# Half down products by token tile, and a per-tile path into the token-head attention, in a two-layer hybrid kernel

## The reference

```python
# experts: top 2 of 8; for each choice e, with its low-rank terms
h  = silu(x @ W1.T + (x @ A1[e].T) @ B1[e].T) * (x @ W3.T + (x @ A3[e].T) @ B3[e].T)
y += gate[e] * (h @ W2.T + (h @ A2[e].T) @ B2[e].T)      # F = 896 = 7 chunks of 128
# heads of a token: q, k, v are [token, 16 heads, 16]; q and k are rotated by the position
scores = einsum('thd,tgd->thg', q, k) / 4 ; w = softmax(scores) ; o = w @ v ; x += o @ Wo.T
```

## Time and profile before

| | |
|---|---|
| median of 3 runs | 1299.37 us (1299.3 to 1304.58) |
| profiled execution, its own time | 1299.7 us |
| its span | 1297.9 us |
| mean granted clock of TensorE | 0.988 |
| busy PE / DVE / ACT / POOL | 1185.8 / 677.1 / 417.7 / 250.0 us |

### The profile page before, as it was taken

One profiled execution on the slowest core, in us unless ns is written; L12 is line 12 of the kernel. 1 busy time (PEld: TensorE's weight loads), 2 busy tenths in 40 slices (PEclk: granted clock), 3 DMA queues, 4 the chain that ended last, 5 costly groups with the idle time before them and its releaser, 6 DMA issues.

```text
span 1297.9 us, 17678 instructions
## 1 busy us (share of the span) xinstructions
PE 1185.8 (91%) x6873; PEld 912.7 (70%) x6873; DVE 677.1 (52%) x1661; ACT 417.7 (32%) x899; POOL 250.0 (19%) x161
## 2 busy tenths in 40 slices
PE   6889999999998989988787999999999989899888
PEld 5678675767867778667665786757678667786666
DVE  5754266664465556344634433666644655563452
ACT  3623031313322342433453431313133223424352
POOL 0002083650110210000000020836501102100000
PEclk9999999999999999999998999999999999999999
DMA  8200000000000000000000000000000000000000
GB/s 348 121 1 1 1 1 1 1 1 1 1 1 2 1 1 1 1 2 9 1 9 1 1 1 1 1 1 1 0 1 1 1 1 1 1 1 2 1 1 17
DMA packets 3570, 17.32 MB, mean 13 GB/s; under 512 B 288, under 2 KB 2464, under 8 KB 2976
## 3 DMA queue, kind: packets, MB, share of 16 engines
q1 hardware_dynamic: 2912, 14.12, 2.7%
q10 hardware_dynamic: 576, 2.08, 0.4%
HBM read 15.15 MB, written 1.05 MB: 12 GB/s over the span
## 4 chain that ended last, share of the span: by engine, by line
PE 69%; DVE 12%; issue 9%; ACT 6%; POOL 3%; DMA 0%; DVEq 0%; POOLq 0%; ACTq 0%
PE bank L704 65%; ACT scr L1311 3%; PE bank L721 2%; DVE XnT L2014 2%; DVE XnT L2016 1%; DVE scr L1590 1%; DVE stat L1582 1%; POOL rstd L2170 1%; DVE negmax L1672 1%; PE bank L822 1%; DVE X L1575 1%; PE bank L1122 1%; ACT scr L1289 1%; POOL fac L2170 1%; ACT XnT L1289 1%
## 5 line engine op out<-in xcount | busy, mean ns | idle before, releaser
L704 PE MATMUL bank<-pack,scr 128*128 128x256 f32 (+2 forms) x952 | 297.7, 464 | 9.4 <-ACT scr L1289 7.5
L704 PE MATMUL bank<-XnT,pack 128*128 128x256 f32 x1024 | 255.4, 390 | 12.3 <-ACT XnT L1289 7.1
L704 PEld LDWEIGHTS bank<-pack,scr 128*128 128x128 f32 x952 | 176.9, 190 | 104.2 <-issue 77.0
L704 PE MATMUL bank<-scr,pack 128*128 128x256 f32 x944 | 227.0, 380 | 1.3 <-DVE scr L1768 1.1
L704 PEld LDWEIGHTS bank<-XnT,pack 128*128 128x128 f32 x1024 | 194.2, 194 | 47.1 <-ACT XnT L1289 9.6
L704 PEld LDWEIGHTS bank<-scr,pack 128*128 128x128 f32 x944 | 178.1, 190 | 30.3 <-issue 4.4
L2205 POOL TENSOR_TENSOR scr<-scr 128x1024 f32<-128x1024 f32 x64 | 149.9, 2390 | 47.3 <-DVEq L1831 46.6
L2170 POOL TENSOR_TENSOR rstd<-veps,half 128x2 f32<-128x2 f32 x32 | 22.3, 698 | 627.1 <-DVE veps L1587 627.1
L1778 DVE TENSOR_TENSOR scr<-bank,scr 128x256 f32<-128x256 f32 x112 | 47.2, 423 | 149.7 <-ACT scr L1362 148.6
L1311 ACT ACTIVATE scr<-bank,negmax 128x256 f32<-128x256 f32 (+1 forms) x256 | 82.9, 445 | 92.8 <-DVE negmax L1672 92.8
L1362 ACT ACTIVATE scr<-bank 128x256 f32<-128x256 f32 x112 | 42.6, 385 | 210.8 <-PE bank L704 210.7
(11 more groups left out here) (184 smaller groups left out, 1406.3 us busy)
## 6 DMA issues: line engine op xcount, KB each, us to landing
pack<-pack_dram SPq DMA_DIRECT2D x1, 6152.0 KB, 17.2
pack<-pack_dram SPq DMA_DIRECT2D x1, 2180.0 KB, 29.2
pack<-pack_dram SPq DMA_DIRECT2D x1, 1595.0 KB, 23.3
X<-x SPq DMA_DIRECT2D x4, 256.0 KB, 16.8
pack<-pack_dram SPq DMA_DIRECT2D x1, 1024.0 KB, 20.2
pack<-pack_dram ACTq DMA_DIRECT2D x1, 975.5 KB, 6.2
pack<-pack_dram SPq DMA_DIRECT2D x1, 793.5 KB, 24.6
out_dram<-X SPq DMA_DIRECT2D x3, 256.0 KB, 2.1
```

Of the source, the lines that this page charges most:

```text
L704: return pe.matmul(o, l, r, start=start, stop=stop, skip_group_check=True)
```

## The change

The order of the stages and their grain change around `middle`; the arithmetic stays the same.

- The down product is split: `down_half` does 3 of the 7 chunks, `down` the other 4, and a stage can be put between them (places "down..h"). For the first experts of a and c the order of the products becomes by tile: (0,0), (1,0), (0,1), (1,1).
- `lora_t`, `lora`, `norm_x(2)`, `norm_t(2)` and `heads_in` go by tile in layer 0. For a and c, tile 0's `lora_t` stands in the middle of the down product (0,1), its `lora` and `norm_x` behind it; for b and d tile 0's `lora_t` stands in the middle of (1,1), its `lora` behind `norm_t(3)`.
- `heads_in` of tile 0 is done before the next experts begin, that of tile 1 at step 2 (a, c) or step 1 (b, d). A second buffer, `rtmp2`, holds the rotation's terms of tile 1. POOL waits for the rotation of the tile that it needs.
- The 16 pieces begin at "f1" in place of "f3" (a, c) or step 1 (b, d), and POOL's first four products at "f0".
- In the first experts of c, `spread_t` of d moves from "down01" to "down10", `spread` and `spread2` from "down10" to "down01h".

```diff
@@ program, first experts of a and of c
-                                  5: [("spread_t", 0, 1)], 6: [("spread", 0, 1), ("spread2", 0, 1)]})
+                                  5: [("spread_t", 0, 1)], 6: [("spread", 0, 1), ("spread2", 0, 1)],
+                                  "down01h": [("lora_t", 0, (0, 0))],
+                                  "down01": [("lora", 0, (0, 0)), ("norm_x", 2, (0, 0))]})
...
-                                  "down01": [("spread_t", 0, d)], "down10": [("spread", 0, d), ("spread2", 0, d)]})
+                                  "down10": [("spread_t", 0, d)],
+                                  "down01h": [("lora_t", 0, (c, 0)), ("spread", 0, d), ("spread2", 0, d)],
+                                  "down01": [("lora", 0, (c, 0)), ("norm_x", 2, (c, 0))]})
@@ middle
             weave[0] = True
+            stage("norm_t", 2, (a, 0))
             stage("x_first", 0, (b, 0))
-            stage("lora", 0, a)
-            stage("norm_x", 2, a)
-            experts(stage, 0, b, token_heads(a))
+            stage("lora", 0, (a, 1))
+            stage("norm_x", 2, (a, 1))
+            stage("heads_in", 0, (a, 0))
+            beside = token_heads(a)
+            beside["down11h"] = [("lora_t", 0, (b, 0))]
+            beside["down11"] += [("lora", 0, (b, 0))]
+            experts(stage, 0, b, beside)
             stage("router", 1, a)
-            stage("lora", 0, b)
+            stage("norm_x", 2, (b, 0))
+            stage("lora", 0, (b, 1))
             stage("spread_t", 1, a)
             stage("top_exp", 1, a)
             stage("spread", 1, a)
-            stage("norm_x", 2, b)
+            stage("norm_t", 2, (b, 0))
+            stage("norm_x", 2, (b, 1))
             stage("spread2", 1, a)
             stage("x_first", 1, (a, 0))
+            stage("heads_in", 0, (b, 0))
             stage("gates", 1, a)
@@ token_heads
             if s % 2 == 0:
-                beside = {"f2": [("norm_t", 2, s)], 2: [("heads_in", 0, s)]}
-                slots = ["f3", 3, "f4", 4, 4, "f5", 5, 5, "f6", 6, 6, "f7", 7, 7, 8, 8]
+                beside = {"f2": [("norm_t", 2, (s, 1))], 2: [("heads_in", 0, (s, 1))]}
+                slots = ["f1", 1, "f2", 2, "f3", 3, "f4", 4, 4, "f5", 5, 5, "f6", 6, "f7", 7]
             else:
-                beside = {"f0": [("norm_t", 2, s)], 0: [("heads_in", 0, s)]}
-                slots = [1, "f2", 2, "f3", 3, 3, "f4", 4, "f5", 5, 5, "f6", 6, 6, "f7", 7]
-            first = 2 if s % 2 == 0 else 0
-            beside[first] += [("head_prod", 0, (s, p)) for p in range(HP)]
+                beside = {"f1": [("norm_t", 2, (s, 1))], 1: [("heads_in", 0, (s, 1))]}
+                slots = ["f1", 1, "f2", 2, "f3", 3, "f4", 4, 4, "f5", 5, 5, "f6", 6, "f7", 7]
+            beside["f0"] = [("head_prod", 0, (s, p)) for p in range(HP)]
@@ experts
-            for i in range(TOPK):
-                for a in range(NT):
-                    stage("down", k, (s, i, a))
-                    others(f"down{i}{a}")
+            tiles = [(i, a) for a in range(NT) for i in range(TOPK)] if k == 0 and s % 2 == 0 else \
+                [(i, a) for i in range(TOPK) for a in range(NT)]
+            for i, a in tiles:
+                stage("down_half", k, (s, i, a))
+                others(f"down{i}{a}h")
+                stage("down", k, (s, i, a))
+                others(f"down{i}{a}")
             summing[0] = False
-            stage("lora_t", k, s)
+            stage("lora_t", k, (s, NT - 1) if k == 0 else s)
@@ PE: one tile's transposes; lora_t(0) has 4 * a filling products, norm_t(2) none
+            def tile_t(key, src, n, idle, ready):
+                o = claim(pe, key)
+                warm(o, idle)
+                pe.wait_ge(*ready)
+                for t in range(n):
+                    last = pe.transpose(o[:, t * P:(t + 1) * P], src[:, t * P:(t + 1) * P], ident)
+                last.then_inc(full[ring.bank(key)], 1)
@@ DVE: one tile's norm
+            def tile_norm(s, a):
+                link(dve.bn_stats(stat[s][:, a, :], X[s][:, a, :]))
+                link(dve.bn_aggr(mv[s][:, a, :], stat[s][:, a, :]))
+                dve.tensor_scalar(veps[s][:, a:a + 1], mv[s][:, a, 1:2], LN_EPS, None, ALU.add)\
+                   .then_inc(tile_var[s], 1)
+                dve.wait_ge(tile_rstd[s], nth(s, 2, a + 1))
+                dve.tensor_scalar(tile_n[s][a], X[s][:, a, :], mv[s][:, a, 0:1], rstd[s][:, a:a + 1],
+                                  ALU.subtract, ALU.mult).then_inc(tile_xn[s], 1)
```

More of the change, by code:

```diff
@@ L51 @@
 SERIES = 8
-NORMS = 8
+NORMS = 7
 H1 = 1024
@@ L315, in hybrid_kernel @@
         am2_ready = each("am2_ready")
+        tile_var = each("tile_var")
+        tile_rstd = each("tile_rstd")
+        tile_xn = each("tile_xn")
         b_in = each("b_in")
@@ L934, in x_second, with down_half @@
                       start=False).then_inc(full[ring.bank(("x", r, m))], 1)
+            summed = set()
+            def down_half(k, sia):
+                s, i, a = sia
+                r = (k, s)
+                wd = w3("m_down", FT)
+                if i == 0 and (r, 0, a) in summed:
+                    return
+                o = claim(pe, ("down", r, i, a))
+                for m in range(FT // 2):
+                    if i == 1 and a == 0:
+                        wait_drained(pe, ("x", r, m))
+                    if i == 1 and a == 0 and joined(k, s):
+                        pe.wait_ge(sum_ready[s], nth_sum(k, s, FT, m + 1))
+                    c0 = D if i == 0 and joined(k, s) else 0
+                    mm(o[:, c0:2 * D], x2T[s][:, i, m, a * P:(a + 1) * P], wd[:, m, c0:2 * D], m == 0, False)
             def down(k, sia):
@@ L939, in down @@
                 wd = w3("m_down", FT)
-                if ("down", r, i, a) in ring.at:
+                if (r, 0, a) in summed and i == 0:
                     return
-                o = claim(pe, ("down", r, i, a))
-                for m in range(FT):
+                o = bank[ring.bank(("down", r, i, a))]
+                for m in range(FT // 2, FT):
                     if i == 1 and a == 0:
@@ L979, in lora, with heads_in @@
                 last.then_inc(full[ring.bank(("lora2", r))], 1)
-            def heads_in(_, s):
-                wait_drained(pe, ("xnT", 2, s))
-                if s == 0:
+            def heads_in(_, sa):
+                s, a = sa
+                wait_drained(pe, ("xnT", 2, s, a))
+                if (s, a) == (0, 0):
                     pe.wait_ge(loaded[3], 16)
                 wqkv = w3("b_wqkv", KD)
[L986 to L994, removed]
+                for name, c0, n in (("bqk", 0, 2 * D), ("bv", 2 * D, D)):
+                    o = claim(pe, (name, s, a))
+                    group(o[:, 0:n], [(XnT[s][:, c, a * P:(a + 1) * P], wqkv[:, c, c0:c0 + n]) for c in range(KD)])\
+                        .then_inc(full[ring.bank((name, s, a))], 1)
             def head_out_t(_, s):
@@ L1808, in lora, with heads_in @@
             def lora(k, s):
+                if k == 0:
+                    s, a = s
+                    key = ("lora2", (k, s), a)
+                    settle()
+                    wait_full(dve, key)
+                    dve.tensor_tensor(X[s][:, a, :], psum(key, D), X[s][:, a, :], ALU.add).then_inc(drain_of(key), 1)
+                    wait_drained(dve, key)
+                    return
                 residual(("lora2", (k, s)), s)
-            def heads_in(_, s):
+            def heads_in(_, sa):
+                s, a = sa
@@ L1831, in heads_in @@
+                ins.then_inc(drain_of(key), 1)
+                wait_drained(dve, key)
+                c, q = (rtmp, rtmp2)[a][s][:, 0], (rtmp, rtmp2)[a][s][:, 1]
+                step(dve.tensor_tensor(rot[s][:, a, :, 0:8], c[:, :, 0:8], q[:, :, 8:16], ALU.subtract))
+                step(dve.tensor_tensor(rot[s][:, a, :, 8:16], q[:, :, 0:8], c[:, :, 8:16], ALU.add))
+                settle()
                 dve.sem_inc(rot_ready[s], 1)
```

106 lines of the change are left out of this document (71 added, 35 removed).

## The result

The changed kernel takes 1310.04 us (median of 8 runs, 1307.82 to 1318.21) where the kernel before takes 1299.34 (8 runs): a ratio of 1.0088, 95% interval 1.0068 to 1.0107. It is slower by 0.9%; the prediction was 1301.5 in a range of 1297.0 to 1306.0, the same within 0.5%. The profiled execution has a span of 1308.2 us, 10.3 more than before.

A forecast was written before the change was run, and what follows sets the result against it. PE, busy 91% of the span, was taken as the bound, with some 12 us of waits to win. 0.1 + 0.5 + 2 x 1.7 - 2 x 0.95 = +2.1 us gave a median of 1301.5 us, range 1297.0 to 1306.0.

The forecast's parts named there:

- The waits of 0.76 and 0.69 before b's heads: Before b's `norm_t` and `heads_in`: both go, 1.77 with tails; about 0.8 returns at tile 1; -0.95 us each for b, d.
- The wait in (1,1): PE stands 1.97 us before tile 0's `lora_t` in b's and d's down product (1,1), for DVE's queued add.
- Tile 1's `lora_t`: Behind down product (1,1) of b and d: the gap of 0.63 becomes 0.37, so -0.26 us.
- a: +0.2 (+0.1): Tile order in a's first experts: gaps of 1.14 together in place of 1.06, so +0.1 us.
- c: +0.8 (+0.5): Tile order in c with d's spread inside: +0.5 us, including a new 0.6 wait for a bank before down (1,1).
- POOL's pieces of a: Start at about 157 in place of 166.9, pause after the fourth, end some 10 us sooner, PE no faster.
- a cover of 5 us. So this costs nothing.: DVE reads `x_second(b, 1)` at about 175.5, PE wants that bank at 180.5, so earlier pieces on POOL cost nothing.
- a wait for a bank in steps 2 to 6: Sign that the prediction is wrong: PE waits in those steps for a bank or for `x2_first`.
- the pieces make DVE late for the banks: Rival, chance 0.1: DVE lags PE beyond the 5 us cover; 2 us more make 8, sum 1309.
- The prediction's worst case by that rule: By DVE and GpSimd's exclusive port lock, each rotated tile's operations are at worst two whole POOL products late, below the cover.
- my bound of 2.6 from the row of L1844: Two two-operand SBUF operations per tile among POOL's products make 0 to 2.6 us of DVE per sequence, inside the cover.
- the sum is one of PE's gaps alone, and each is worked out at its place.: Products, transposes, filling products and pieces stay the same in number, so only PE's gaps were summed, to +2.1 us.

The follow-up runs named there:

- e2: The changed kernel with `gates(1, a)` put back ahead of `heads_in(b, 0)`: median 1307.71 us, ratio 1.0072 to the kernel before.
- e4: The kernel before with one thing altered, `gates(1, a)` moved behind `heads_in(b)` at step 0: median 1304.00 us, ratio 1.0037.
- e1: The changed kernel with the name `down_half` given banks 0 to 3 in `lanes`: median 1309.45 us, ratio 1.0074 to the kernel before.
- e10: e9 with `lora_t` of b (layer 0), a (layer 1) and partners also behind the next router and `spread_t`, without filling products: 1294.47 us, ratio 0.9947.
- e8: e7 with the whole `lora_t` of a and c behind `x_first(b, 0)`, without filling products: median 1299.23 us, ratio 0.9987 to the kernel before.
- e9: e8 with DVE's add as a stage of its own directly behind the last down product's read: median 1294.86 us, ratio 0.9970 to the kernel before.
- e6: Changed kernel with `down_half` in banks 0-3, `gates` before `heads_in(b, 0)`, b/d tile 0 `lora_t` before `head_out`, and pieces at their old places: 1305.96 us, ratio 1.0044.
- e11: The changed kernel with only the 16 pieces back in the places of the kernel before: median 1314.70 us, ratio 1.0100 to the kernel before.
- e7: The kernel before with `norm_t(2)`, `heads_in` and the pieces of b and d at the places of a and c: 1298.89 us, ratio 0.9997.

## Why the prediction was wrong

**What held.** The waits of 0.76 and 0.69 before b's heads are gone, and 0.53 came back at tile 1: from `x_first(1, (a, 0))` to the end of b's `heads_in` -1.2 (forecast -0.95). The wait in (1,1): 1.69 shown, 1.85 with its tail (1.97). Tile 1's `lora_t`: 0.21 shown, 0.37 with its tail (0.37). a: +0.2 (+0.1). c: +0.8 (+0.5), with the bank wait as forecast; only the sizes were off. These make about +1.8 (0.2 + 0.8 + 2 x (1.85 - 0.26 - 1.2)), where the sum said +2.1. POOL's pieces of a start at 156.0 (about 157), pause 2.0 after the fourth and end 8.9 sooner (some 10), and PE is no faster for it.

**What failed, first: "a cover of 5 us. So this costs nothing."** I worked the cover out for a's pieces and took it for all four sequences. In b's and d's, `gates` now runs beside POOL. I had read the price of such an operation from L1844, 849 to 1705 ns, and counted the rotation's two; the gates' were not counted, since their line in the diff is not marked as moved. They cost 8 us on DVE, past the cover, and PE waits 1.66 and 1.57 with the tail for the bank (e2 takes 3.5 in all away, e4 makes 3.0 alone). This is the sign that the prediction itself named as showing it wrong: a wait for a bank in steps 2 to 6. The rival "the pieces make DVE late for the banks" named the place and the point from which it decides; it had 0.1, and its mechanism was half right: not the pieces' places but an older stage that fell behind the start of POOL. The rule of the Trainium skill ("SBUF — State Buffer", "Who interferes with whom") that the second to start stands still to the other's end is borne out: 2.05 us for 160 ns of work, and in e2 two operations with 4.4 us. The prediction's worst case by that rule, two whole products for a tile or 4.7 us, holds for the rotation's 3.5 more; my bound of 2.6 from the row of L1844 does not.

**What failed, second: "the sum is one of PE's gaps alone, and each is worked out at its place."** The banks of `down_half` were not looked at: for c I asked which of three banks was late, for b and d not. A stage's name decides its banks in `lanes`, and a new name took the default. That is 1.2 us with its tail before each `norm_t(3)` (e1: 2.7 in all).

**The sum again.** 1.8 foreseen, 3.2 for the gates, 2.4 for the name, and 0.3 for the wait for ACT before the four `head_out`s (0.76 for 0.69), which goes with the name too (e1): 7.7 of the 8.2 us in P1 and P2. The last 0.5 has no place of its own. So the number was missed by two terms that the sum did not have, not by the sizes of those that it had.

**The clock.** The stretches of unchanged work are 2.3 us longer in this trace. Their rows answer to the earlier trace rows:

```profile
320.70:743.20 422.50, 374.96 (x2507) 299.22 (x2506) 209.16 (x540) 158.96 (x362) 36.99 (x29) 0.97 0.01 2
973.50:1308.20 334.70, 302.42 (x1967) 242.05 (x1965) 163.45 (x418) 113.91 (x262) 33.41 (x23) 0.98 0.01 2
```

The last stretch has 0.98 where it had 0.99. Over the profiles of all kernels here the middle stretch, with the same instructions, takes 454.7 to 461.1 us and the last 337.0 to 342.7. Runs of the kernel before at a mean granted clock of 0.988 have a median of 1299.7 (1297.8 to 1303.7), two of the changed kernel at 0.988 take 1307.8 and 1308.2: 8.3 us, what P1 and P2 say. The rest of the measured 10.7 goes with the clock: the changed kernel's 8 runs had 0.984 in the mean, the kernel before 0.987 to 0.988. Why an order of stages should get a lower clock was not settled; the other altered kernels lie at 0.982 to 0.988.

**Left open.** The order by tile of a and c was not undone alone; its +0.2 and +0.8 are read from the traces. Whether the filling products that e10 leaves out keep the clock up was not tried by itself; e10 has the lowest mean clock, 0.982.

## What to carry to other kernels

In a program whose engines each run one fixed order, a stage put in costs also through what now stands behind it: walk every engine's list past the insertion, the lines that the diff doesn't mark too, and ask which engine the new stage starts. A piece of work to cover a wait must be ahead on the waiting engine only; if it is one stage on all engines, it delays the very thing that is waited for, and the stage has to be split (e8 against e9). A wait can cost more than its own length, since the clock may be lower behind it (e6, e11). A new name or key in a table with a default is a change of resources.

## What the runs showed of the hardware

Among POOL's products of 2.35 us, DVE's `tensor_scalar` and `tensor_tensor` on SBUF alone waited for the running product to end, whatever their size: a `tensor_scalar` of 128x2 took 2350 ns (158 to 170 without POOL), a `tensor_tensor` of 128x2 2048 ns (160), two `tensor_tensor` of 128x256 took 1.84 and 2.56 us (0.42). A reciprocal of 128x2 between them took 0.17, the reductions of 128x1024 1.21 and reads of a PSUM bank 0.42 as ever, and POOL's products kept their 2.35 us. So, measured by their own length, short operations on DVE lose most beside POOL.

Behind an idle of TensorE of 2.71 us (e6) and 2.25 us (e11) its granted clock stood at 0.50 for some 3.5 us, which cost 1.69 us each time in P1; behind one of 1.69 us it stayed at 1.00.

The mean granted clock of one and the same kernel differs from run to run (0.978 to 0.995 for the kernel before). Over all runs of the thirteen kernels a straight line gives 0.86 us for each 0.001. For a question of 2 us, stretches of one trace told more here than ratios of medians: e7 has 3.8 us less in P1 and P2 and a ratio of 0.9997.
